# Another order of the eight row tiles in each attention sequence of a mixture-of-experts attention kernel

## The reference

```
xn = layernorm(x)                                   # x is [4, 1024, 512]
# attention: normalised again, with gamma and beta
q, k, v = x_norm @ qkv[:, :512], x_norm @ qkv[:, 512:1024], x_norm @ qkv[:, 1024:]
scores  = where(causal, q @ k.T / sqrt(512), -inf)  # for each sequence
s       = softmax(scores) @ v @ o_proj + xn
# experts: softmax router, the two best of 8, silu(x @ wg) * (x @ wu) @ wd, and a shared expert
g       = silu(routed + shared)
out     = x + s * g
```

## Time and profile before

| | us |
|---|---|
| median of 3 runs | 1262.59 (1261.72 to 1263.6) |
| the profiled execution, its own time | 1259.98 |
| its span in the trace | 1258.2 |
| TensorE busy in the span | 1176.6 (94%) |
| VectorE, ScalarE, GpSimd busy | 598.5, 456.3, 343.9 |
| stage 4 | 863 to the end |

### The profile page before, as it was taken

How to read it: one execution, slowest core, us unless ns; L and a number is a source line. 1 busy time by engine, 2 the same in 40 slices (tenths; PEclk the granted TensorE clock), 3 DMA queues, 4 the chain that set the end, 5 groups by cost and what they waited for, 6 DMA issues and landing times. The chain is left out here.

```text
span 1258.2 us, 21972 instructions
## 1 busy us (share of the span) xinstructions
PE 1176.6 (94%) x6958; PEld 653.6 (52%) x6959; DVE 598.5 (48%) x1198; ACT 456.3 (36%) x822; POOL 343.9 (27%) x430
## 2 busy tenths in 40 slices
PE   5899999999999559999999999997899999999996
PEld 3455555556565235555555555553444444454443
DVE  5555555555555831112112211225765776776455
ACT  4433333333332112222222222223553553554452
POOL 1030000000001431212221221212554564565653
PEclk9899999999999769999999999998999999999999
DMA  8567666766674149977777777765268368257364
GB/s 298 165 161 188 168 165 179 192 166 164 178 187 107 44 92 255 218 188 174 175 183 178 174 179 179 174 153 174 76 151 225 92 149 237 85 123 204 106 146 109
DMA packets 324802, 206.44 MB, mean 164 GB/s; under 512 B 263168, under 2 KB 271368, under 8 KB 324368
## 3 DMA queue, kind: packets, MB, share of 16 engines
q1 hardware_dynamic: 313920, 170.39, 54.1%
q0 software_dynamic: 10800, 35.40, 10.8%
q10 hardware_dynamic: 32, 0.02, 0.0%
HBM read 96.88 MB, written 45.88 MB: 113 GB/s over the span
## 5 line engine op out<-in xcount | busy, mean ns | idle before, releaser
L444 PE MATMUL pair<-arena 128*128 (+1 forms) x3240 | 509.6, 314 | 13.1 <-DMA arena<-arena 13.1
L444 PEld LDWEIGHTS pair<-arena 128*128 128x128 f16 x3240 | 316.2, 98 | 193.0 <-issue 15.0
L451 PE MATMUL bank<-arena 128*128 (+1 forms) x1215 | 289.9, 385 | 8.9 <-ACT arena L884 5.1
L451 PEld LDWEIGHTS bank<-arena 128*128 128x128 f16 x1215 | 119.9, 99 | 138.8 <-issue 13.1
L1265 DVE SCALAR_TENSOR_TENSOR arena<-pair,arena 128x352 f32<-128x352 f32 x71 | 37.2, 525 | 269.9 <-ACT arena L1237 266.1
L1517 PE MATMUL pair<-arena 128*128 128x512 f16 x672 | 154.1, 385 | 2.9 <-PEq L1122 2.9
L1237 ACT ACTIVATE arena<-pair 128x352 f32<-128x352 f32 x71 | 33.0, 464 | 214.5 <-PE pair L444 214.5
L1517 PEld LDWEIGHTS pair<-arena 128*128 128x128 f16 x672 | 66.6, 99 | 78.9 <-issue 7.4
L1545 PE MATMUL bank<-arena 128*128 128x512 f16 x432 | 98.6, 379 | 7.9 <-DMA arena<-arena 7.9
L201 POOL TENSOR_TENSOR root_seed<-var_eps,minus_half 128x1 f32<-128x1 f32 x32 | 17.6, 551 | 318.6 <-DVE var_eps L210 318.5
L1532 PE MATMUL pair<-arena 128*128 128x512 f16 (+3 forms) x576 | 98.9, 326 | 1.1 <-ACT arena L1589 1.1
(11 more groups left out here) (164 smaller groups left out, 1162.0 us busy)
## 6 DMA issues: line engine op xcount, KB each, us to landing
arena<-in_L_attn_x_dram SPq DMA_DIRECT2D x96, 256.0 KB, 3.4
slot_rows<-arena SPq DMA_DIRECT2D x71, 256.0 KB
xn_rows<-arena SPq DMA_DIRECT2D x32, 256.0 KB, 2.4
shared_rows<-arena SPq DMA_DIRECT2D x32, 256.0 KB, 2.6
arena<-shared_rows SPq DMA_DIRECT2D x32, 256.0 KB, 2.9
out_dram<-arena SPq DMA_DIRECT2D x32, 256.0 KB, 3.3
arena<-in_L_ffn_wg_dram SPq DMA_DIRECT2D x32, 176.0 KB, 3.0
arena<-in_L_ffn_wu_dram SPq DMA_DIRECT2D x32, 176.0 KB, 3.4
```

Source lines behind the costliest of these rows:

```text
L444: last = pe.matmul(bank[:, 0:H], xt[:, a, c, :], weights(c, b, col), start=(c == 0 and i == 0), stop=(c == KC - 1 and i == 2))
L451: last = pe.matmul(bank[:, :], ht[:, a, c, :], weights(c, b), start=(start and c == 0 and i == 0), stop=(stop and c == HC - 1 and i == 2))
```

## The change

Only the list of the tile order is written otherwise:

```diff
-            ORDER = list(range(1, QT, 2)) + list(range(QT - 2, -1, -2))
+            ORDER = list(range(QT // 2 - 1, QT, 2)) + [QT - 2, QT // 2] + list(range(QT // 2 - 2, -1, -1))
```

## The result

| | before | changed |
|---|---|---|
| median, 13 executions each | 1260.99 us | 1265.29 us |
| ratio, with its 95% interval | | 1.0045 (1.0028 to 1.0063) |
| span of the profiled execution | 1258.2 | 1261.0 |
| start of stage 4 in it | 863.16 | 860.84 |
| length of stage 4 in it | 395.0 | 400.2 |

The changed kernel is slower by 0.45%, about 5.7 us, where +5.9 was forecast. The medians lie 4.3 apart. The forecast time was 1268.5, which is 3.2 too high; 1.6 of that is that the kernel before itself came out lower than in its first three executions. One of the 13 executions before took 1571 us and is left out of the ratio. In the two profiled executions stage 4 is 5.2 us longer; the stages ahead of it, which the change leaves alone, happened to take 2.3 us less, so the spans differ by 2.8 only.

What follows compares the result with a forecast made beforehand. TensorE was taken to bound the kernel, with only its stalls able to change: -1.1 + 0.3 + 0 + 5.3 + 1.4 = +5.9 us. Added to 1262.59 this gave 1268.5 us, range 1261.5 to 1273.5.

Steps and rivals of the forecast that it cites:

- The frame: Stage 4: TensorE, busy 92.75 of 96 us in one sequence, sets the time; its work stays, only its stalls change.
- Part 1, S2: Scores of position 2, waiting for the exponential of position 0: the 0.27 us stall goes in four sequences, -1.1 us.
- Part 2, W2: Weighing of position 2, waiting for its larger transpose T2: slightly longer stalls in two sequences, +0.3 us.
- Part 3, W4: Weighing of position 4: cover falls from 16 units to 12, but its transpose just fits, 0 us.
- Part 4: Weighings W5 and W6, sequences 0 to 2: transpose T6, held by GpSimd and SyncE, makes TensorE wait 3.4 us each, +5.3.
- rival C: Late positions' needs shrink with their tiles, T6 comes early enough: no change, 1262.1 us; chance 0.14.
- Part 5: End of sequence 3: weighings W5, W6 and W7 stall 3.6 us together against 2.16 before, +1.4 us.
- A: Transpose T2 grows with all of its 8.4 us, +2.15 at W2 in nearly every sequence: about 1277 us; chance 0.07.
- B: TensorE's clock falls behind the 3.4 us stalls in sequences 0 to 2, 4.9 us more: 1273.4 us; chance 0.10.
- D: As rival C, and T2 escapes the gather and small last tiles cover their end: faster, 1259.5 us; chance 0.07.

## Why the prediction was right, point by point

**The frame** held: TensorE sets the time, its work is the same, and the sum of the stalls moved by 5.3 where stage 4 moved by 5.2.

**Part 1, S2**, came out as worked: all four stalls are gone.

**Part 2, W2**, was mis-sized: +0.3 forecast, +2.1 measured. The issue of T2 was right (0.1 later). The term that was off is the landing: +0.65 taken, +1.2 measured in the mean of the four sequences (and up to +1.9 in one, so that sequences 1 and 2 lost their slack and stalled too). The slope from 4 and 10 blocks is not what failed, since T3 of 16 blocks landed in 4.3 where T2 of 12 landed in 3.7. What failed is "the excess is the gather's, which does not grow": beyond the price of the blocks, the landing grew by another 0.6 us. It goes with T2's new place among the gather's two DMAs, but why is not shown. The gather was named rightly as what makes T2 slow.

**Part 3, W4**: no stall, as forecast.

**Part 4** was right in sign and mis-sized: 3.4 per sequence forecast, 2.4, 2.9 and 2.1 measured, so +2.4 in place of +5.3. T6 left W2's end after 15.2 to 15.5 us, not 16.9, and landed in 3.4 to 3.9, not 2.7. The chain up to the mix shrank by 2.2 in sequence 1 and not by 0.9: mix began 6.9 us after W2's end (1050.70 against 1043.84), where it had been 9.0 (1049.53 against 1040.50, both ends taken at the next row's start). The term left out is again VectorE's. The last step of `combine` behind W2, in sequence 1 before and after:

```profile
1041.66 1.91 DVE L1690 SCALAR_TENSOR_TENSOR arena<-arena 128x512 f32<-128x512 f32 x1
```
```profile
1045.01 0.69 DVE L1690 SCALAR_TENSOR_TENSOR arena<-arena 128x512 f32<-128x512 f32 x1
```

Before, it ran beside GpSimd's `finish` (1041.92 to 1043.01); after, `finish` had ended at 1044.26. That is 1.2 of the 2.2, and the narrower operations are the 0.95 as worked. And the cause I named was only part of it. The run with T6 ahead of the store shows that the order on SyncE delays T6's issue by 0.3 at most and its landing by about 1. What holds T6's issue, and all of W5's stall in the new order, is VectorE's `combine` and low half beside GpSimd: with the mix moved away T6 goes out 13.3 us after W2's end and W5's stall is gone. I had priced the slow low half (1.90 us) as relief in rival C, not as a cause that stays.

**Part 5** was right within 0.5 in its sum, 4.1 against 3.6 forecast, by errors that partly cancel: W5, W6 and W7 stalled 1.2, 1.9 and 1.0 where 0.6, 1.3 and 1.7 were forecast. W5's share of 1.2 is again VectorE's slowed low half, since it vanished when the mix moved to position 4.

**The sum** of +5.9 against +5.3 by stalls is closer than its terms: part 2 was 1.8 too low, part 4 2.9 too high, part 5 0.5 too low. That they cancel to 0.6 is luck. What was not luck is the frame and the sign of each part.

**The rivals.** A, T2 growing in proportion, was part true: +1.2 on top of 8.0, where it asked for 2.8 and I for 0.65. That is twice the 0.6 that the four blocks cost with no gather close by, the least that taking turns with the gathers would make of it; no run shows that this is the cause. B, the clock, didn't happen in the changed kernel, but is real: it came behind single stalls of 3.2 to 4.0 in one run, and behind stalls of 2.3 to 2.5 in the old order. C was half true: W5 stalled 1.2 in each sequence, near its 1.4, as T5 landed in 2.8 and not in the 4.4 that I counted, and T6 went out 0.35 us behind its low half in sequence 1. But it needed the chain 2 us shorter than counted, which came out 1.4 to 1.7 shorter, and W6 without a stall, which was 0.9 to 1.7. D fell: W2 stalled more, not less.

## What to carry to other kernels

When work is reordered under a bounding engine, write for each wait its need (issue after what, and time to land) against its cover (what the engine does meanwhile): that bookkeeping foretold a new order's stalls to about a tenth. But then ask of each need what makes it long. Here much of it was GpSimd's additions slowing VectorE and gathers queued close to a transpose. Moving those took the order stalls from 14.3 to 3.2 us and gave 0.6% against the kernel before, and three orders of the tiles then came out within 1.2 us of each other.

## What the runs showed of the hardware

- A DMA transpose in on-chip memory of 6, 10, 12, 14 and 16 blocks of 128x128 landed in 2.8, 3.4, 3.7, 4.0 and 4.3 us at its quickest, with no gather issued close to it (12 blocks: a gather 1.3 us behind it, and 5.3 in sequence 0 of three runs, 6.0 once). That is 0.15 us a block. 16 blocks with a gather 0.3 us behind landed in 5.6.
- Two gather DMAs of 256 KB, the first 0.6 to 1.7 us ahead of the transpose and the second between 0.2 ahead and 1.3 behind, made 6 blocks take 6.2 to 6.9, 12 blocks 7.2 to 9.1 (5.6 once) and 16 blocks 8.8 to 11.1 us. With both further ahead (2.7 and 1.2 us) 10 blocks took 4.0 to 4.1. With the first 0.3 us behind the transpose, 6 blocks took their 2.8, but 10 blocks 5.0 to 6.1 in sequences 0 and 1 and 3.4 in sequence 2.
- VectorE's operations with two operands in on-chip memory take longer while GpSimd's run: 0.55 us became 1.62, 0.69 became 1.91 and 2.17. The Trainium skill ("SBUF — State Buffer", SBUF: two separate sides) says that the two engines share a pair of ports as a lock, held for a whole instruction. The 2.17 fits that: it ended 0.56 us after GpSimd's addition, nearly its own length of 0.69.
- TensorE's clock fell behind single stalls of 2.25, 2.43, 2.51 and 2.55 us and not behind others of 2.49, 2.52 and 2.58. Where it fell, the next 4 us ran at a granted 0.57 to 0.68, and the matmuls cost 1.5 to 1.7 us more. Behind stalls of 3.2 to 4.0 they cost 1.7 to 2.8 more.
